# Layer 3's four-bit MLP: two batches rounded together, part of the elementwise work given to GpSimd and ScalarE

## The chip, the cores and the metric

The kernel runs on one core of one Trainium2 chip. The metric is the time of one execution on the device, in microseconds (us), input loads and the store of the output included. Five engines work side by side, each from its own queue in order, and wait for each other by semaphores: TensorE (PE; its weight loads are PEld), VectorE (DVE), ScalarE (ACT), GpSimd (POOL), SyncE (SP, which issues the DMAs). "Idle before" in a row of the profile is time in which the engine stood still.

## What is computed

A decoder of four layers on 8 batches of 112 rows by 256 columns. The change touches only the last stage, the feed-forward part of layer 3, where inputs, hidden values and weights are rounded to four-bit numbers with one scale for each block of 16:

```python
def fake_quant_nvfp4(x, global_scale):
    xb = x.reshape(..., 16)
    amax = max(abs(xb))                      # of each block
    sc8 = round_to_e4m3(clip(amax / 6 * global_scale, 0, 448))
    dq = sc8 / global_scale
    a = clip(abs(xb) / dq, 0, 6)
    return sign(xb) * nearest_fp4(a) * dq

x = x + down(fake_quant(silu(gate(fake_quant(xn))) * up(fake_quant(xn))))   # hidden width 1024
```

## The kernel before

Twelve stages follow each other; `L3Ffn` is the last, and between stages all engines meet (`open_stage`, `close_stage`). Weights are rounded earlier (`FourBitWeights`, in a stage of layer 2, the same helpers at 128 partitions x 2048).

The stage works on ten units of 112 partitions x 1024 floats: `rows` 0 and 1 (the normalized inputs of batches 0 to 3 and of 4 to 7) and `hidden` 0 to 7 (one batch each). `order()` gives the order of steps; each engine's method walks the same list and emits its own part, so a step's place in the list is its place in each engine's queue.

For a unit ("four"), DVE does: the blocks' largest magnitude (L3185, a reduction to 64), nine small operations on 64 numbers a partition that make the scale and its inverse (`four_bit_scales`), and then on 1024 elements: multiply by the inverse scale, clip, take the exponent's bits, make the rounding constant, add it (`four_bit_sums`), and subtract it again (L3373). `Chain` lets each of them wait for the one before (tensor_tensor is L2731, tensor_scalar L2737 or L2735, the reciprocal L2749). POOL multiplies the rounded values by the scale into bf16 (`four_bit_values`, L3176). PE transposes them in 8 blocks (`pe_turn`, L3422), ACT copies them out of PSUM (L3439 for rows, L3444 for hidden), and for a hidden unit PE does the down projection (L259, 8 matmuls of 256 columns), whose result DVE scales and adds to `x` (L3376).

"gate" is, for a batch, eight matmuls of 512 columns on PE (gate into banks 0 and 1, up into banks 2 and 3), ACT's silu of the gate half into `sg` (L3433), and DVE's product with the up half, read from PSUM (L3357). `k.fill` lets PE wait until a bank's reader is done; here banks 0 to 3 are free once DVE's product is.

In the loop over batches DVE's queue is: reduction, small operations, six operations on 1024 elements for batch b, the gate product of batch b + 1, the sum of batch b - 1. `y`, `t`, `hids`, `sc` and `values` are buffers; `t` is a single one.

Of the kernel before, what the change touches and what calls it, by code (L numbers as in the profile page):

```python
# [5 lines left out]
F32 = mybir.dt.float32  # L6
# [41 lines left out]
class Signals:  # L48


    def __init__(self, nc, stack):
# [95 lines left out]
        self.sums_ready = new("sums_ready")  # L147
        self.xl_ready = new("xl_ready")
# [3024 lines left out]
def four_bit_values(k, values, y, sc):  # L3173

    b3 = lambda a: a.rearrange("p (n k) -> p n k", k=16)
    return k.nc.gpsimd.tensor_tensor(b3(values), b3(y),  # L3176
                                     sc[:, 1].unsqueeze(2).broadcast_to([y.shape[0], sc.shape[2], 16]), ALU.mult)


def four_bit_scales(k, src, gs, sc):  # L3180

    c, V, s = Chain(k), k.nc.vector, k.s
    top, s8, c8 = sc[:, 0], sc[:, 1], sc[:, 2]
    V.wait_ge(*s.vstep.now())
    V.tensor_reduce(top, src.rearrange("p (n k) -> p n k", k=16), AX, ALU.max,  # L3185
                    apply_absolute_value=True).then_inc(*s.vstep.up())
# [11 lines left out]
def four_bit_sums(k, src, y, t, sc):  # L3198

    c = Chain(k)  # L3200
    b3 = lambda a: a.rearrange("p (n k) -> p n k", k=16)
    c.tt(b3(y), b3(src), sc[:, 2].unsqueeze(2).broadcast_to([y.shape[0], sc.shape[2], 16]), ALU.mult)
# [3 lines left out]
    c.tt(y, y, t, ALU.add)  # L3206
# [89 lines left out]
class L3Ffn:  # L3296
# [4 lines left out]
    UNITS = (("rows", 0), ("rows", 1)) + tuple(("hidden", b) for b in range(B))  # L3301

    def __init__(self, k):
# [8 lines left out]
        self.values = [take(HID, dt=BF16, parts=S) for _ in range(2)]  # L3312
        self.sg, self.hids = take(HID, parts=S), take(2, HID, parts=S)
        self.hT = take(8, S, dt=BF16)

    def order(self):

        yield "norm", B - 1
        yield "four", 0
        yield "four", 1  # L3320
        yield "turn", 0
        yield "gate", 0
        yield "turn", 1
        for b in range(B):
            yield "four", b + 2
            if b + 1 < B:
# [4 lines left out]
        yield "sum", B - 1  # L3331

    def rows_of(self, n):
        kind, i = self.UNITS[n]
        if kind == "rows":
            half = self.k.row_norms[:, i * HALF:(i + 1) * HALF, :]
            return half.rearrange("p b d -> p (b d)"), self.w["s_in"][0:S, 0:1]
        return self.hids[:, i % 2, :], self.w["s_in"][0:S, 1:2]
# [10 lines left out]
    def dve(self):  # L3349
        k, s, V, st = self.k, self.s, self.nc.vector, self.k.stats  # L3350
        V.tensor_copy(self.ident16, k.ident).then_inc(*s.wq_ready.up())
        for step, i in self.order():
            if step == "norm":
                norm_row_stats(k, i, st, s.stat_ready)
            elif step == "gate":
                V.wait_ge(*s.silu_ready(i + 1))
                V.scalar_tensor_tensor(  # L3357
                    out=self.hids[:, i % 2, :].rearrange("p (h n) -> p h n", h=2), in0=k.banks[0:S, 2:4, :],
                    scalar=self.inv[0:S, 1:2], in1=self.sg.rearrange("p (h n) -> p h n", h=2), op0=ALU.mult,
                    op1=ALU.mult).then_inc(*s.hid_ready.up())  # L3360
            elif step == "four":
                kind, b = self.UNITS[i]
                if kind == "hidden":
                    V.wait_ge(*s.hid_ready(b + 1))
                elif b:
                    V.wait_ge(*s.xn_ready(1))
                if i >= 2:
                    V.wait_ge(*s.quant_ready(i - 1))
                src, gs = self.rows_of(i)
# [313 lines left out]
```

## Time and profile before

| | us |
|---|---|
| median of three runs | 2364.27 (2362.84 to 2365.53) |
| the profiled execution | 2364.53, its span 2363.2 |
| the last stage, in the profile | 2240.9 to 2358.3 |
| DVE busy over the whole span | 1354.9 (57%) |
| PE busy over the whole span | 2043.6 (86%) |

Over the whole span PE is the busiest engine, but the last stage has another balance; the rows below are read from it. The share of each engine in one stage, the queue of its busiest engine and what each of the others waits for tell what a change inside this stage can be worth.

### The profile page before, as it was taken

Reading aid. Unit: us, or ns where it says so; the run is one execution under the profiler, and the core shown is the slowest. Engines: PE = TensorE matmul, PEld = TensorE weight load, DVE = VectorE, ACT = ScalarE, POOL = GpSimd, SP = SyncE. Lnnn points to the kernel's source line nnn. Section 1 sums busy time; section 2 is a strip of 40 time slices with the busy share of each in tenths; the row PEclk is TensorE's granted clock in tenths of the full one; section 3 lists DMA queues with packets and bytes.
Section 4 is the critical chain, followed back from the end, with each engine's and each line's share of the span. In section 5 each row is a group of like instructions: output and inputs, shape, how many; then the busy total and the mean of one; then the engine's idle time right before and its main releaser. Section 6 shows DMA issues by size and latency. Waiting matters only on the chain.

```text
span 2363.2 us, 57229 instructions
## 1 busy us (share of the span) xinstructions
PE 2043.6 (86%) x22720; PEld 1483.5 (63%) x22720; DVE 1354.9 (57%) x3605; ACT 883.8 (37%) x3421; POOL 500.9 (21%) x1131
## 2 busy tenths in 40 slices
PE   7999999998987799897976887999999998789843
PEld 3788888786656566465865654666554544556522
DVE  5666666674335688544644633787263210678797
ACT  2344444443236466211333532666210111246511
POOL 3344444221001100101324511332000000411111
PEclk9655555799989899799997998999999999789966
DMA  3000000104000000300011000000030000000000
GB/s 133 3 5 5 5 4 5 75 2 175 3 1 2 14 12 5 134 1 23 1 48 81 2 1 7 11 8 5 1 148 0 1 0 1 1 14 15 2 0 16
DMA packets 7752, 57.20 MB, mean 24 GB/s; under 512 B 760, under 2 KB 5216, under 8 KB 5728
## 3 DMA queue, kind: packets, MB, share of 16 engines
q1 hardware_dynamic: 7488, 53.54, 5.9%
q8 instruction: 183, 3.00, 0.5%
q14 instruction: 81, 0.66, 0.1%
HBM read 52.62 MB, written 0.92 MB: 23 GB/s over the span
## 4 chain that ended last, share of the span: by engine, by line
PE 66%; DVE 14%; issue 9%; ACT 6%; POOL 4%; DMA 1%; DVEq 0%; POOLq 0%; ACTq 0%; SPq 0%
PE banks L259 42%; PE banks L264 8%; PE banks L1323 6%; PE banks L908 3%; ACT memory L956 2%; DVE memory L1421 2%; PE banks L934 2%; ACT memory L1352 1%; PE banks L1474 1%; ACT memory L1359 1%; DVE memory L1218 1%; DVE memory L795 1%; DVE memory L1427 1%; DVE memory L1430 1%; DVE memory L1439 1%
## 5 line engine op out<-in xcount | busy, mean ns | idle before, releaser
L259 PE MATMUL banks<-memory 128*112 128x256 f32 (+7 forms) x4192 | 1134.2, 427 | 70.7 <-ACT memory L3444 8.0
L259 PEld LDWEIGHTS banks<-memory 128*128 128x128 f32 (+3 forms) x4192 | 708.2, 196 | 401.5 <-issue 258.9
L264 PE MATMUL banks<-memory 112*125 112x112 f32 (+3 forms) x2000 | 305.9, 286 | 123.7 <-DVE memory L795 66.7
L264 PEld LDWEIGHTS banks<-memory 112*125 112x125 f32 (+3 forms) x2000 | 238.6, 172 | 240.3 <-issue 142.9
L1323 PE MATMUL banks<-memory 128*128 128x8 bf16 (+2 forms) x10752 | 325.9, 175 | 25.6 <-DVE memory L1439 5.8
L1323 PEld LDWEIGHTS banks<-memory 128*128 128x128 bf16 x10752 | 304.2, 104 | 48.0 <-DVE memory L1439 45.9
L956 ACT ACTIVATE memory<-banks,memory 112x375 f32<-112x375 f32 x384 | 215.4, 579 | 19.5 <-DVE memory L994 19.1
L994 DVE TENSOR_REDUCE memory<-banks 112x2 f32<-112x750 f32 x192 | 171.0, 933 | 37.0 <-PE banks L908 36.8
L811 POOL TENSOR_TENSOR memory<-memory 112x1 f32<-112x1 f32 x72 | 39.6, 550 | 416.1 <-DVE memory L790 414.6
L1002 DVE COPY memory<-banks 125x448 f32<-125x448 f32 x192 | 116.8, 619 | 11.3 <-PE banks L264 6.9
L1421 DVE TENSOR_REDUCE memory<-banks 128x48 f32<-128x192 f32 x448 | 109.4, 286 | 5.5 <-PE banks L1323 5.5
L908 PE MATMUL banks<-memory 32*112 32x375 f32 x768 | 88.4, 529 | 19.6 <-ACT memory L956 17.4
L1502 ACT ACTIVATE memory<-memory 112x112 f32<-112x112 f32 x192 | 71.7, 374 | 86.1 <-DVE memory L1523 86.1
L1352 ACT ACTIVATE memory<-memory 128x48 f32<-128x48 f32 x224 | 54.4, 243 | 128.1 <-DVE memory L1421 128.1
L978 ACT COPY memory<-banks 125x448 f32<-125x448 f32 x96 | 51.1, 533 | 127.6 <-PE banks L264 127.6
L3142 DVE TENSOR_TENSOR memory<-banks,memory 112x256 f32<-112x256 f32 x8 | 3.4, 424 | 158.4 <-PE banks L259 158.4
L1383 POOL TENSOR_TENSOR memory<-memory 128x16 f32<-128x16 f32 x224 | 48.2, 215 | 206.4 <-DVE memory L1439 206.4
L1201 ACT ACTIVATE memory<-banks,memory 112x112 f32<-112x112 f32 x256 | 86.4, 391 | 9.5 <-DVE memory L1218 8.1
L1366 ACT COPY banks<-memory 128x48 f32<-128x48 f32 x448 | 79.8, 179 | 23.9 <-DVE memory L1400 23.9
L3119 ACT ACTIVATE memory<-banks,memory 128x448 f32<-128x448 f32 x32 | 20.3, 635 | 173.5 <-PE banks L259 173.5
L1439 DVE SCALAR_TENSOR_TENSOR memory<-memory 128x16 f32<-128x16 f32 x224 | 39.2, 175 | 75.7 <-ACT memory L1359 75.7
L956 ACT ACTIVATION_READ_ACCUMULATOR memory<-banks,memory 112x1 f32 x384 | 80.4, 209 | 0.0
(233 smaller groups left out, 2403.8 us busy)
## 6 DMA issues: line engine op xcount, KB each, us to landing
memory<-in_l2x SPq DMA_DIRECT2D x1, 7680.0 KB, 21.5
memory<-in_l2f SPq DMA_DIRECT2D x1, 7168.0 KB, 19.8
memory<-in_l1f SPq DMA_DIRECT2D x1, 4617.0 KB, 14.1
memory<-in_ctxT SPq DMA_DIRECT2D x24, 187.5 KB
memory<-in_l0a SPq DMA_DIRECT2D x1, 4224.0 KB, 16.5
memory<-in_l2f SPq DMA_DIRECT2D x1, 4096.0 KB, 12.8
memory<-in_l3f SPq DMA_DIRECT2D x1, 3073.0 KB, 22.5
memory<-in_l2a SPq DMA_DIRECT2D x1, 3072.0 KB, 18.4
```

The costliest lines, as they stand in the source:

```text
L259: ins = self.nc.tensor.matmul(out, weights[i], acts[i], start=i == 0, stop=i == n - 1)
L264: return self.nc.tensor.transpose(out, in_, self.ident[0:n, 0:n])
L908: ins = PE.matmul(k.bank(bank, S, CK), q, kT, start=True, stop=True)
L956: self.nc.scalar.activation(self.P_both[gi % 2][:, r, :], self.k.bank(r, S, CK), ACT.Exp, bias=u["nmax"][:, 4 * i + r:4 * i + r + 1], scal ...
L994: V.tensor_reduce(u["nmax"][:, 4 * i + 2 * h:4 * i + 2 * h + 2], k.banks[0:S, 2 * h:2 * h + 2, 0:CK], AX, ALU.max, negate=True).then_inc(* ...
L1002: V.tensor_copy(self.PT_both[gi % 2][0:CR, c, :], k.bank(k.at["turn", gi, c], CR, 4 * S)).then_inc(*s.pt_v.up())
L1201: A.activation(self.P_all[:, i, g, :], k.bank(i, S, 4 * S)[:, g * S:(g + 1) * S], ACT.Exp, bias=u["nmax"][:, 4 * i + g:4 * i + g + 1], sca ...
L1323: ins = self.nc.tensor.matmul(own[:, part:3, at:at + B], whh[:, part, l, j, g * P:(g + 1) * P], self.upper[l][:, 0:3 - part, j * B:(j + 1) ...
L1352: A.activation(self.gates[:, l, 1:4, :].rearrange("p g c -> p (g c)"), self.sums[:, l, 0:6 * B], ACT.Tanh).then_inc(*s.act_tanh.up())
L1366: self.nc.scalar.copy(self.slots[l][last][:, 3, :], src).then_inc(*self.s.xw_in.up())
L1421: V.tensor_reduce(self.sums[:, l, first * B:end * B], self.slots[l][last].rearrange("p s c -> p c s"), AX, ALU.add).then_inc(*s.gates_in.up())
L1502: A.activation(weights, weights, ACT.Exp, bias=self.nmax[n % 2][:, at:at + 1], scale=1.0, accum_out=self.total[n % 2][:, at:at + 1]).then_ ...
```

## The change

- `hids`, `y` and `t` become two buffers each of 2048 floats, `sc` two of 3 x 128. Two hidden batches form a pair.
- DVE: the reduction (`four_bit_tops`) stays one for each batch ("hid"); the nine small operations now run once for a pair on 128 numbers ("scale"), as do the multiplication by the inverse scale and the three operations of `four_bit_range` on 2048 elements ("range"). The addition of the rounding constant stays one of 1024 for each batch ("round").
- POOL: the gated product (`up` times `sg`, both in SBUF) in the place of DVE's L3357; the subtraction of the rounding constant for all units but rows 0 and the last; then the values as before, except those of the last unit.
- DVE keeps subtraction and values of the last unit (`last_ready`).
- ACT: after the silu a scaled copy of the up half out of PSUM into `up`; banks 0 to 3 are free once that is done (`up_ready`). `sg` and `up` are single buffers: the next silu waits for POOL's product.
- PE: transposes alternate between banks 4 and 5; `hT` is double. The order of steps is new; POOL's queue is product, product, then for the pair subtraction, values, subtraction, values.

```diff
-        self.y, self.t = [take(HID, parts=S) for _ in range(2)], take(HID, parts=S)
-        self.sc = [take(3, HID // 16, parts=S) for _ in range(2)]
+        two = lambda *dims, dt=F32: [take(*dims, dt=dt, parts=S) for _ in range(2)]
+        self.hids, self.y, self.t = two(2 * HID), two(2 * HID), two(2 * HID)
...
         yield "norm", B - 1
-        yield "four", 0
-        yield "four", 1
+        yield "rows", 0
+        yield "rows", 1
         yield "turn", 0
         yield "gate", 0
-        yield "turn", 1
-        for b in range(B):
-            yield "four", b + 2
-            if b + 1 < B:
-                yield "gate", b + 1
-            if b:
-                yield "sum", b - 1
+        yield "hid", 0
+        yield "gate", 1
+        yield "hid", 1
+        for p in range(HALF):
+            last = p == HALF - 1
+            yield "scale", p
+            if not last:
+                yield "gate", 2 * p + 2
+                yield "hid", 2 * p + 2
+            if p:
+                yield "turn", 2 * p
+            if not last:
+                yield "gate", 2 * p + 3
+            yield "turn", 2 * p + 1
+            yield "range", p
+            if not last:
+                yield "hid", 2 * p + 3
+            yield "round", p
+            if p:
+                yield "sum", 2 * p - 2
+                yield "sum", 2 * p - 1
+        for b in (B - 2, B - 1):
...
         for step, i in self.order():
             if step == "norm":
                 norm_row_stats(k, i, st, s.stat_ready)
...
-            elif step == "gate":
-                V.wait_ge(*s.silu_ready(i + 1))
-                V.scalar_tensor_tensor(
-                    out=self.hids[:, i % 2, :].rearrange("p (h n) -> p h n", h=2), in0=k.banks[0:S, 2:4, :],
-                    scalar=self.inv[0:S, 1:2], in1=self.sg.rearrange("p (h n) -> p h n", h=2), op0=ALU.mult,
-                    op1=ALU.mult).then_inc(*s.hid_ready.up())
-            elif step == "four":
...
+            elif step == "rows":
+                if i:
                     V.wait_ge(*s.xn_ready(1))
...
+                src = k.row_norms[:, i * HALF:(i + 1) * HALF, :].rearrange("p b d -> p (b d)")
+                y, t = self.half(self.y, i), self.half(self.t, i)
+                four_bit_scales(k, src, w["s_in"][0:S, 0:1], self.scales(i))
+                four_bit_scaled(k, src, y, self.scales(i))
+                four_bit_range(k, y, t)
+                self.dve_round(i, i == 0)
+            elif step == "hid":
+                self.dve_hidden(i)
+            elif step == "scale":
+                sc = self.sc[i % 2]
+                if i:
+                    V.wait_ge(*s.quant_ready(2 * i))
+                four_bit_steps(k, w["s_in"][0:S, 1:2], sc)
+                four_bit_scaled(k, self.hids[i % 2], self.y[i % 2], sc)
+            elif step == "range":
+                four_bit_range(k, self.y[i % 2], self.t[i % 2])
+            elif step == "round":
+                self.dve_round(2 * i + 2, False)
+                self.dve_round(2 * i + 3, 2 * i + 3 == self.LAST)
...
+    def dve_hidden(self, b):
+        k, s, V = self.k, self.s, self.nc.vector
+        hid = self.half(self.hids, b + 2)
+        V.wait_ge(*s.hid_ready(b + 1))
+        four_bit_tops(k, hid, self.scales(b + 2)[:, 0])
+
+    def dve_round(self, n, whole):
+
+        k, s, V = self.k, self.s, self.nc.vector
+        y, t = self.half(self.y, n), self.half(self.t, n)
+        V.wait_ge(*s.vstep.now())
+        if not whole:
+            V.tensor_tensor(y, y, t, ALU.add).then_inc(*s.sums_ready.up())
+            return
+        V.tensor_tensor(y, y, t, ALU.add).then_inc(*s.vstep.up())
+        V.wait_ge(*s.vstep.now())
+        V.tensor_tensor(y, y, t, ALU.subtract).then_inc(*s.sums_ready.up())
+        if n == self.LAST:
+            V.wait_ge(*s.sums_ready(n + 1))
+            V.wait_ge(*s.tp16_full(n - 1))
+            four_bit_values(V, self.values[n % 2], y, self.scales(n)[:, 1]).then_inc(*s.last_ready.up())
...
-            elif step == "four":
-                G.wait_ge(*s.sums_ready(i + 1))
-                if i >= 2:
-                    G.wait_ge(*s.tp16_full(i - 1))
-                four_bit_values(k, self.values[i % 2], self.y[i % 2], self.sc[i % 2]).then_inc(*s.quant_ready.up())
+            elif step == "rows" and i == 0:
+                self.pool_values(0)
+            elif step == "hid":
+                G.wait_ge(*s.up_ready(i + 1))
+                if i >= 4:
+                    G.wait_ge(*s.sums_ready(i - 1))
+                G.tensor_tensor(self.half(self.hids, i + 2), self.up, self.sg, ALU.mult).then_inc(*s.hid_ready.up())
+                if i == 0:
+                    self.pool_values(1)
+            elif step == "round":
+                self.pool_values(2 * i + 2)
+                if 2 * i + 3 < self.LAST:
+                    self.pool_values(2 * i + 3)
+
+    def pool_values(self, n):
+        s, G, y = self.s, self.nc.gpsimd, self.half(self.y, n)
+        G.wait_ge(*s.sums_ready(n + 1))
+        if n:
+            G.tensor_tensor(y, y, self.half(self.t, n), ALU.subtract).then_inc(*s.gstep.up())
+            G.wait_ge(*s.gstep.now())
+        if n >= 2:
+            G.wait_ge(*s.tp16_full(n - 1))
+        four_bit_values(G, self.values[n % 2], y, self.scales(n)[:, 1]).then_inc(*s.quant_ready.up())
...
-                        k.fill(o + h, s.hid_ready(i + 1))
+                        k.fill(o + h, s.up_ready(i + 1))
...
-        PE.wait_ge(*s.quant_ready(n + 1))
-        k.fill(bank, read)
+        PE.wait_ge(*(s.last_ready(1) if n == self.LAST else s.quant_ready(n + 1)))
...
                 A.activation(self.sg.rearrange("p (h n) -> p h n", h=2), k.banks[0:S, 0:2, :], ACT.Silu,
-                             scale=self.inv[0:S, 0:1]).then_inc(*s.silu_ready.up())
+                             scale=self.inv[0:S, 0:1])
+                A.activation(self.up.rearrange("p (h n) -> p h n", h=2), k.banks[0:S, 2:4, :], ACT.Copy,
+                             scale=self.inv[0:S, 1:2]).then_inc(*s.up_ready.up())
```

## Rows read from the trace of the kernel before

**Rows 1.** The stage: window, length; busy us of PE, PEld, DVE, ACT, POOL; granted clock.
```profile
2240.90:2358.30 117.40, 49.24 (x208) 31.82 (x208) 106.45 (x181) 19.26 (x19) 21.09 (x12) 0.60 0.00 0
```

**Rows 2.** Groups of the stage by shape: busy us, mean ns, idle before, releaser.
```profile
L2731 DVE TENSOR_TENSOR memory<-memory 112x1024 f32<-112x1024 f32 x20 | 24.5, 1225 | 0.7
L3176 POOL TENSOR_TENSOR memory<-memory 112x1024 bf16<-112x1024 f32 x10 | 19.3, 1930 | 90.6 <-DVE memory L3373 90.6
L2737 DVE TENSOR_SCALAR memory<-memory 112x1024 f32<-112x1024 f32 x20 | 13.9, 694 | 0.7
...
L3185 DVE TENSOR_REDUCE memory<-memory 112x64 f32<-112x1024 f32 x10 | 12.1, 1210 | 0.1
L3357 DVE SCALAR_TENSOR_TENSOR memory<-banks,memory 112x1024 f32<-112x1024 f32 x8 | 10.2, 1277 | 0.0
...
L3433 ACT ACTIVATE memory<-banks,memory 112x1024 f32<-112x1024 f32 x8 | 8.9, 1115 | 34.5 <-PE banks L259 34.5
```

**Rows 3.** Groups by shape, whole span: the same operations at doubled width, in `FourBitWeights`.
```profile
L2731 DVE TENSOR_TENSOR memory<-memory 128x2048 f32<-128x2048 f32 x9 | 20.6, 2292 | 0.3
...
L2737 DVE TENSOR_SCALAR memory<-memory 128x2048 f32<-128x2048 f32 x6 | 7.4, 1227 | 0.2
...
L2749 DVE RECIPROCAL memory<-memory 128x128 f32<-128x128 f32 x3 | 2.9, 954 | 0.1
...
L2737 DVE TENSOR_SCALAR memory<-memory 128x128 f32<-128x128 f32 x9 | 2.4, 268 | 0.3
...
L2731 DVE TENSOR_TENSOR memory<-memory 128x128 f32<-128x128 f32 x6 | 1.8, 293 | 0.2
```

**Rows 4.** Groups by shape of POOL, whole span: f32 tensor_tensor of two plain inputs.
```profile
L2894 POOL TENSOR_TENSOR memory<-memory 128x448 f32<-128x448 f32 x8 | 9.0, 1134 | 27.0 <-ACT memory L2885 27.0
...
L2030 POOL TENSOR_TENSOR memory<-memory 128x224 f32<-128x224 f32 x8 | 5.2, 655 | 22.0 <-DVE memory L1236 22.0
```

**Rows 5.** Timeline, four places where POOL and DVE overlap: start us, duration us, engine.
```profile
986.07 2.23 POOL L2894 TENSOR_TENSOR memory<-memory 128x448 f32<-128x448 f32 x2 [4.20 <-ACT memory L2885]
...
986.64 1.67 DVE L2731 TENSOR_TENSOR memory<-memory 112x32 f32<-112x32 f32 x2
...
2021.88 0.62 DVE L2573 TENSOR_TENSOR memory<-memory 112x448 f32<-112x448 f32 x1 [1.81 <-ACT memory L2536]
...
2021.92 1.57 POOL L2573 TENSOR_TENSOR memory<-memory 112x448 f32<-112x448 f32 x1 [1.23 <-ACT memory L2536]
...
2242.71 1.22 POOL L3170 TENSOR_SCALAR memory<-memory 112x256 f32<-112x256 f32 x1
2243.05 0.26 DVE L2737 TENSOR_SCALAR memory<-memory 112x64 f32<-112x64 f32 x1
...
2251.88 1.93 POOL L3176 TENSOR_TENSOR memory<-memory 112x1024 bf16<-112x1024 f32 x1 [7.94 <-DVE memory L3373]
2252.96 0.90 DVE L2737 TENSOR_SCALAR memory<-memory 112x64 f32<-112x64 f32 x1
```

**Rows 6.** Timeline: the first gate, and the subtraction of the second hidden batch.
```profile
2256.01 3.66 PE L259 MATMUL banks<-memory 128*112 128x512 bf16 x8 [1.05 <-ACT memory L3439]
...
2282.93 1.22 DVE L3373 TENSOR_TENSOR memory<-memory 112x1024 f32<-112x1024 f32 x1
```

**Rows 7.** Timeline of the end, from the last subtraction to the last sum.
```profile
2350.58 1.22 DVE L3373 TENSOR_TENSOR memory<-memory 112x1024 f32<-112x1024 f32 x1
...
2351.89 1.93 POOL L3176 TENSOR_TENSOR memory<-memory 112x1024 bf16<-112x1024 f32 x1 [9.34 <-DVE memory L3373]
...
2353.87 0.93 PE L3422 MATMUL banks<-memory 112*128 112x112 bf16 x8 [7.40 <-POOL memory L3176]
2354.84 0.91 ACT L3444 COPY memory<-banks 128x896 bf16<-128x896 bf16 x1 [10.37 <-PE banks L3422]
...
2355.80 1.95 PE L259 MATMUL banks<-memory 128*112 128x256 bf16 x8 [0.99 <-ACT memory L3444]
2357.79 0.48 DVE L3376 SCALAR_TENSOR_TENSOR memory<-banks,memory 112x256 f32<-112x256 f32 x1 [5.58 <-PE banks L259]
```

More of the change, by code:

```diff
@@ L147, in __init__ @@
         self.sums_ready = new("sums_ready")
+        self.last_ready = new("last_ready")
+        self.up_ready = new("up_ready")
         self.xl_ready = new("xl_ready")
@@ L3170, in norm_row, with four_bit_values, four_bit_tops @@
     return G.tensor_scalar(k.row_norms[:, b, :], k.x[:, b, :], st[:, 6:7], st[:, 9:10], ALU.subtract, ALU.mult)
-def four_bit_values(k, values, y, sc):
+def four_bit_values(engine, values, y, s8):
     b3 = lambda a: a.rearrange("p (n k) -> p n k", k=16)
[L3176 to L3183, printed above, removed]
+    return engine.tensor_tensor(b3(values), b3(y), s8.unsqueeze(2).broadcast_to([y.shape[0], s8.shape[1], 16]), ALU.mult)
+def four_bit_tops(k, src, top):
+    V, s = k.nc.vector, k.s
     V.wait_ge(*s.vstep.now())
@@ L3186, in four_bit_scales, with four_bit_steps @@
                     apply_absolute_value=True).then_inc(*s.vstep.up())
+def four_bit_scales(k, src, gs, sc):
+    four_bit_tops(k, src, sc[:, 0])
+    four_bit_steps(k, gs, sc)
+def four_bit_steps(k, gs, sc):
+    c = Chain(k)
+    top, s8, c8 = sc[:, 0], sc[:, 1], sc[:, 2]
     c.ts(top, top, 1.0 / 6.0, gs, ALU.mult, ALU.mult)
@@ L3198, in four_bit_sums, with four_bit_scaled, four_bit_range @@
 def four_bit_sums(k, src, y, t, sc):
+    four_bit_scaled(k, src, y, sc)
+    four_bit_range(k, y, t)
+    Chain(k).tt(y, y, t, ALU.add)
+def four_bit_scaled(k, src, y, sc):
+    b3 = lambda a: a.rearrange("p (n k) -> p n k", k=16)
+    Chain(k).tt(b3(y), b3(src), sc[:, 2].unsqueeze(2).broadcast_to([y.shape[0], sc.shape[2], 16]), ALU.mult)
+def four_bit_range(k, y, t):
     c = Chain(k)
-    b3 = lambda a: a.rearrange("p (n k) -> p n k", k=16)
-    c.tt(b3(y), b3(src), sc[:, 2].unsqueeze(2).broadcast_to([y.shape[0], sc.shape[2], 16]), ALU.mult)
     c.ts(y, y, 6.0, -6.0, ALU.min, ALU.max)
@@ L3308, in __init__ @@
         self.ident16 = take(P, dt=BF16)
-        self.y, self.t = [take(HID, parts=S) for _ in range(2)], take(HID, parts=S)
-        self.sc = [take(3, HID // 16, parts=S) for _ in range(2)]
+        two = lambda *dims, dt=F32: [take(*dims, dt=dt, parts=S) for _ in range(2)]
+        self.hids, self.y, self.t = two(2 * HID), two(2 * HID), two(2 * HID)
+        self.sc = two(3, 2 * HID // 16)
         self.xT = four_bit_rows(k)
-        self.values = [take(HID, dt=BF16, parts=S) for _ in range(2)]
@@ L3313, in __init__ @@
-        self.sg, self.hids = take(HID, parts=S), take(2, HID, parts=S)
-        self.hT = take(8, S, dt=BF16)
+        self.values = two(HID, dt=BF16)
+        self.sg, self.up = take(HID, parts=S), take(HID, parts=S)
+        self.hT = [take(8, S, dt=BF16) for _ in range(2)]
     def order(self):
         yield "norm", B - 1
-        yield "four", 0
-        yield "four", 1
+        yield "rows", 0
+        yield "rows", 1
         yield "turn", 0
         yield "gate", 0
-        yield "turn", 1
@@ L3340, in run, with half, scales @@
+        for b in (B - 2, B - 1):
+            yield "turn", b + 2
+        for b in (B - 2, B - 1):
+            yield "sum", b
+    def half(self, a, n):
+        pair = a[(n // 2 + 1) % 2]
+        return pair[:, n % 2 * self.HID:(n % 2 + 1) * self.HID]
+    def scales(self, n):
+        return self.sc[(n // 2 + 1) % 2][:, :, n % 2 * self.HID // 16:(n % 2 + 1) * self.HID // 16]
     def run(self):
@@ L3439, in act @@
                     A.copy(self.xT[:, b].rearrange("p k (b s) -> p b k s", b=HALF),
[L3440 removed]
+                           self.turned(4 + i % 2).rearrange("p (b k) s -> p b k s", b=HALF)).then_inc(*s.xT_ready.up())
                 else:
[L3442 to L3444 removed]
+                    if b >= 2:
+                        A.wait_ge(*s.down_full(b - 1))
+                    A.copy(self.hT[b % 2], self.turned(4 + i % 2)).then_inc(*s.h_kept.up())
 def fetch_l0_l1(k):
```

38 lines of the change are left out of this document (9 added, 29 removed).

## Prediction, made before the changed kernel was seen

> **What bounds the kernel now.** Only the last stage changes, so its own rows decide. The busy times of the stage come first: of 117.4 us DVE is busy 106.5, PE 49.2, POOL 21.1, ACT 19.3 [rows 1]. The groups by shape say what DVE does and that it hardly waits (0.7 us before twenty operations), while POOL stood 90.6 us idle for DVE's last operation on a unit [rows 2]. From the subtraction that starts at 2282.93 (second hidden batch) to the one at 2350.58 (the eighth) 67.65 us pass [rows 6, 7]: six batches, 22.55 us a pair, on one full queue. At the end come 6.5 us from the end of the last subtraction (2351.80) to the end of the last sum (2358.27) [rows 7].
>
> **What DVE gives away.** For a pair it loses two gated products of 1.28 and two subtractions of 1.22, 5.0 us. Doubling the width saves little more: one multiplication is 2.29 for twice 1.225, one clip 1.23 for twice 0.69 [rows 2, 3]. What is left for a pair: two reductions 2.42; small operations of 128 numbers, six tensor_scalars (0.23 to 0.27, together 1.45), two tensor_tensors 0.59, one reciprocal 0.95, so 3.0; multiplication 2.29; range 3 x 1.23 = 3.68; two additions 2.45; two sums 0.95 [rows 2, 3, 7]; some 0.3 of gaps and overlaps are over. That is 15.1 instead of 22.55.
>
> **What POOL takes.** Values cost 1.93 [rows 2]. Product and subtraction, 1024 f32 from two plain inputs, are not in the trace. From below: 1.93, the values. From above: 655 ns for 224 and 1134 for 448 are 2.14 ns an element, so 1.134 + 576 x 2.14 ns = 2.37 [rows 4]. I take 2.3, near the plain rows. The Trainium skill (GPSIMD Engine Reference, 3.1 Elementwise) measures 4497 ns for 2048; half of it, 2.25, is an estimate and would shorten the sum by about 0.7 us; no run here shows it. POOL then has per pair 4 x 2.3 + 2 x 1.93 = 13.1 us. Beside DVE's 15.1 that would fit, if the two ran side by side.
>
> **They do not.** Where POOL's values op runs from 2251.88 to 2253.81, DVE's tensor_scalar on 64 numbers, issued at 2252.96, takes 0.90 us instead of 0.26 and ends 0.05 after POOL. Two tiny tensor_tensors beside two POOL operations take 1.67 us, where even 128-wide ones take 0.29 each: one gets through after each POOL operation. The other way round, POOL's 448 elements behind a DVE tensor_tensor take 1.57 instead of 1.13 [rows 3, 4, 5]. So a DVE operation with two inputs in SBUF, or a tensor_scalar, and a POOL operation exclude each other, in order of arrival; only start-up is shared (about 0.15 to 0.2 of a blocked DVE operation, 0.13 of a blocked POOL one). DVE's reductions (memory to memory, one input) and its products out of PSUM keep means of 1.21 and 1.28 though the values op lies beside them in every batch [rows 2]. This is what the change gives up: POOL works now just where it disturbs nobody; afterwards it disturbs clips, additions and small operations. The Trainium skill (SBUF, Who interferes with whom) says that the one that comes second waits out the whole instruction; the rows give back the start-up. By the rule alone, some 20 hand-overs would cost 3 us more, 2379.
>
> **A pair, placed.** Zero is the end of the pair's second addition. POOL: first subtraction to 2.2 (its start-up was over while it waited), beside it the two sums (free). Then values 4.2, second subtraction 6.5, values 8.4, next product 10.7; in each gap one small DVE operation gets through, so five of nine are done at 10.9, the rest, free, at 12.7. Multiplication to 15.0; the other product (its gate: PE until 12.0 behind the transposes and projection that the first values release, ACT until 14.2) waits for it, 17.2; the reduction lies beside it; the first range operation waits until 17.2 and ends at 18.2, the others at 20.75; reduction 21.9, additions 23.1 and 24.3. So 24.3 instead of 22.55: ten of POOL's 13.1 us come on top of DVE's 15.1, and of the rest start-up is most. The last interval has no products and no reductions: about 19.2. Together 24.3 + 24.3 + 19.2 = 67.8 against 67.65: **plus 0.2**.
>
> **The head.** Rows 0 and the first gate stay (PE until 2259.67, silu 1.11 [rows 2, 6]). ACT's copy of up is not in the trace; silu on the same shape is 1.11, and it is hidden wherever POOL is behind; here it is on the path. Then POOL: product 0 from 2262.0 to 2264.3, subtraction and values of rows 1 to 2268.6, product 1 to 2270.9: DVE, done with rows 1 at 2260.9, waits 8 us in all for the two products and reduces batch 1 until 2272.2. Small operations 3.3 and, since product 2 falls into them (second gate done 2265.6, ACT 2267.9; third gate 2271.5, ACT 2273.8), 2.2 more, to 2277.6; multiplication 2279.9; reduction 2281.1; product 3 until 2282.1 delays the range, 2285.9; reduction and two additions 2289.2. Before, the same point was 2284.15: **plus 5.0**.
>
> **The tail.** From the last addition: subtraction of batch 6 on POOL 2.2, values, behind DVE's subtraction of batch 7, to 5.1; DVE's own values of batch 7 are done at 6.2, hidden. But PE takes the two batches in turn: transposes 0.93, copy 0.91, projection 1.95 and their gaps, 3.9, then the same 3.9 for batch 7, and a sum 0.48: 5.1 + 3.9 + 3.9 + 0.5 = 13.4 against 6.5 [rows 7]: **plus 6.9**. Before, the other batch of this pair had gone out 11 us earlier.
>
> Edits with one answer: banks 4 and 5 in turn, the double `hT`, the split of the scales' helper: nothing, PE is busy 49 of 117 us [rows 1]. Banks 0 to 3 are free after ACT's copy rather than after DVE's product; PE waits for DVE anyway. The added waits: behind POOL's wait for `up_ready` stand the values of rows 1 (counted in the head) and later the pair's subtractions, which are due after it anyway; behind DVE's for `hid_ready` stands its whole queue, which the head and the pair count; its wait for `quant_ready` asks for values of two pairs ago.
>
> **The sum.** 5.0 + 0.2 + 6.9 = 12.1. The profiled execution took 2364.53, 0.3 above the median 2364.27; so **2376.4**. With product and subtraction at 1.93, each pair is 1.3 to 1.5 shorter, head and tail 1.5 together: about 5 less, 2371.6.
>
> **The rivals.**
> (a) Exclusion, forecast: slower, 2371 to 2380. For it stand rows of both orders and both kinds of DVE operation [rows 5].
> (b) Faster. DVE and POOL run side by side at this size: Then not DVE's 15.1 but the other product sets the pair. From the end of the first addition: subtraction 2.3, values 4.4, transposes, copy and projection 8.3, gate 11.9, ACT 14.2, product 16.5, reduction 17.7, addition 19.0. So 19.0, 19.0 and 12.6 for the last, 17.0 less than 67.65; in the head product 2 and 3 delay nothing and additions end at 2285.5, plus 1.3; in the tail 1.9 less waiting, plus 5.0: minus 10.7, **2353.8**. It decides if less than about half of POOL's time shuts DVE out. Against it stands the 0.90 for 0.26 [rows 5].
> (c) Between. POOL holds DVE off only in part of an operation: a DVE tensor_scalar issued 0.34 us into POOL's L3170 (1.22) ran in its free 0.26 [rows 5]. That one is a POOL tensor_scalar, with one input. If half of POOL's time is open for DVE, half of the way between (a) and (b): 2365, **no change**.
> (d) The copy on ACT makes table loads (one only for the stage now, copies and silu mixed) or is far longer than 1.11: ACT has 98 us to spare [rows 1], so only the head would feel it; under 2 us, inside (a).
>
> **How the numbers follow.** Chances: (a) 0.76, (b) 0.12, (c) 0.12. A time within 0.2% (4.7 us) can't be told from no change. (a) leaves slower 0.75 and 0.01 for same; so faster 0.12, same 0.13, slower 0.75. The range takes in (a) with its low price of 1.93, a gentler order of arrival at the port (3 us less), and the rule's 2379 with PE's gates and copies a little later (4 more), and reaches down to (c)'s middle: 2364 to 2383.
>
> **What the profile after would show.** Small tensor_scalars of 128 numbers with a mean near 1 us instead of 0.25; POOL's product and subtraction at 2.3 free and about 3 where they wait for an addition; DVE busy more, not less, than 106.5 us; additions of neighbouring pairs 24.3 us apart; 13.4 us from the last plain addition to the last sum. If the small operations show 0.2 to 0.3 and pairs are 19 apart, (b) is true and the argument of the port is wrong; if product and subtraction take 1.9, only a size is off.

## The result and the profile after

The changed kernel takes 2376.47 us (median of five, 2373.76 to 2384.67) against 2365.53 us for the kernel before on the same chip (five, 2362.84 to 2367.57). The ratio is 1.0053, with a 95% interval of 1.0032 to 1.0073: slower, by 10.9 us between the medians. 2376.4 was predicted. Ratios, here and below, are worked out from all runs of both kernels and so are not exactly the quotient of two medians. One later execution of the kernel before took 4326.7 us, in a slow state of the chip, and is left out of every comparison.

The profiled execution is the longest of the five, 2384.67 us, so first one has to see where its time lies. Its span is 2383.3 us, 20.1 longer than the 2363.2 of before. The stage begins with the cast of the identity on DVE, at 2240.92 before and at 2247.95 now: 7.0 us of the 20.1 are there before the first changed instruction. One place at which they arise is a view of five us early in the program, in the same unchanged code (columns as in rows 1: window, length, busy us of PE, PEld, DVE, ACT, POOL, granted clock). Before:

```profile
455.00:460.00 5.00, 5.00 (x47) 4.17 (x48) 3.99 (x10) 3.41 (x17) 1.47 (x2) 1.00 0.01 2
```

After:

```profile
455.00:460.00 5.00, 5.00 (x20) 3.88 (x19) 1.87 (x4) 3.29 (x17) 0.00 (x0) 0.50 0.00 2
```

PE is busy all five us in both, but the granted clock was 0.50 instead of 1.00, the lower instead of the higher of its two levels, and it got through 20 instead of 47 matmuls (the two stretches don't hold quite the same ones). One reciprocal of DVE starts at 451.76 before and at 451.94 after, and the one two rounds of this code later at 464.74 and 468.56. So 3.6 of the 7.0 us arise here, the rest further on in code that is unchanged too. A second profile of the changed kernel (below) has the low clock at this place too (2.2 us lost), but its stage begins 1.0 us earlier than that of before. So such losses come and go with the execution.

What belongs to the change is the stage itself, from that cast to the end of the last sum: 117.35 us before (2240.92 to 2358.27), 130.46 after (2247.95 to 2378.41). Windows of after: the whole stage, and the stage cut at the end of the first pair's additions and at the end of the last plain addition:

```profile
2247.95:2378.41 130.46, 46.82 (x208) 30.17 (x208) 112.74 (x114) 26.95 (x27) 65.39 (x27) 0.57 0.00 0
...
2247.95:2296.45 48.50, 18.92 (x56) 9.00 (x56) 37.92 (x56) 13.57 (x13) 18.99 (x10) 0.54 0.00 0
2296.45:2365.20 68.75, 22.32 (x120) 16.55 (x120) 66.99 (x53) 11.57 (x12) 41.41 (x17) 0.60 0.00 0
2365.20:2378.41 13.21, 5.58 (x32) 4.63 (x32) 7.83 (x6) 1.81 (x2) 4.98 (x2) 0.50 0.00 0
```

Before, the same three parts were 43.23 (2240.92 to the subtraction's end at 2284.15), 67.65 and 6.47 [rows 6, 7]. So the stage grew by 5.3 + 1.1 + 6.7 = 13.1 us. DVE executes 114 instructions in it instead of 181 and is busy for 112.7 us instead of 106.5 [rows 1]: fewer and wider operations, more time (the time for which a started operation is held up counts as busy). The groups of after by shape say which (busy us, mean ns, idle before, releaser):

```profile
L2739 DVE TENSOR_SCALAR memory<-memory 112x128 f32<-112x128 f32 x12 | 13.1, 1092 | 0.3
...
L2733 DVE TENSOR_TENSOR memory<-memory 112x128 f32<-112x128 f32 x8 | 8.5, 1064 | 0.3
...
L2737 DVE TENSOR_SCALAR memory<-memory 112x128 int32<-112x128 int32 x4 | 7.0, 1758 | 0.1
```

The operations on 128 numbers take 1.1 to 1.8 us on average instead of the 0.27 and 0.29 of [rows 3]. The two kinds of POOL work and the copy that moved to ACT, from the same view:

```profile
L3456 POOL TENSOR_TENSOR memory<-memory 112x1024 f32<-112x1024 f32 x8 | 23.3, 2909 | 18.6 <-ACT memory L3519 18.6
L3468 POOL TENSOR_TENSOR memory<-memory 112x1024 f32<-112x1024 f32 x8 | 22.4, 2799 | 28.6 <-DVE memory L3435 28.6
...
L3519 ACT ACTIVATE memory<-banks,memory 112x1024 f32<-112x1024 f32 x8 | 8.9, 1107 | 0.0
```

How a pair runs is read from DVE's and POOL's timeline after the first pair's additions (start, duration):

```profile
2295.39 3.25 POOL L3468 TENSOR_TENSOR memory<-memory 112x1024 f32<-112x1024 f32 x1 [6.27 <-DVE memory L3435]
2296.36 2.36 DVE L2739 TENSOR_SCALAR memory<-memory 112x128 f32<-112x128 f32 x1
2298.72 1.93 POOL L3178 TENSOR_TENSOR memory<-memory 112x1024 bf16<-112x1024 f32 x1
2298.76 4.27 DVE L2737 TENSOR_SCALAR memory<-memory 112x128 f32<-112x128 f32 x2
2300.61 2.34 POOL L3468 TENSOR_TENSOR memory<-memory 112x1024 f32<-112x1024 f32 x1
...
2303.03 1.93 POOL L3178 TENSOR_TENSOR memory<-memory 112x1024 bf16<-112x1024 f32 x1
2303.07 1.97 DVE L2739 TENSOR_SCALAR memory<-memory 112x128 f32<-112x128 f32 x1
2304.91 2.35 POOL L3456 TENSOR_TENSOR memory<-memory 112x1024 f32<-112x1024 f32 x1
2305.07 2.66 DVE L2733 TENSOR_TENSOR memory<-memory 112x128 f32<-112x128 f32 x2
...
2309.55 4.29 POOL L3456 TENSOR_TENSOR memory<-memory 112x1024 f32<-112x1024 f32 x1 [2.29 <-ACT memory L3519]
```

Read the two engines together: from 2295.4 to 2307.3 POOL works through five operations with gaps under 0.1, and one small DVE operation ends just after each of them (a row marked x2 holds two). The last row is the reverse: a product whose free time is 2.34 takes 4.29, since DVE's multiplication of 2048 (2309.34 to 2311.63) came first.

### The profile page after: what moved, and what is told of

The parts are those of the page before. It is cut to its first block, busy times and chain, and to the rows that moved or that the text cites. A ratio compares the mean times of both kernels' runs of the same rounds, so it can differ in the third digit from the quotient of the medians.

```text
span 2383.3 us, 57191 instructions
## 1 busy us (share of the span) xinstructions
PE 2046.1 (86%) x22720; PEld 1483.3 (62%) x22720; DVE 1361.9 (57%) x3538; ACT 890.5 (37%) x3429; POOL 544.6 (23%) x1146
## 4 chain that ended last, share of the span: by engine, by line
PE 66%; DVE 14%; issue 7%; ACT 7%; POOL 5%; DMA 1%; DVEq 0%; POOLq 0%; ACTq 0%; SPq 0%
PE banks L261 42%; PE banks L266 7%; PE banks L1325 6%; PE banks L910 3%; ACT memory L958 2%; DVE memory L1423 2%; PE banks L936 2%; ACT memory L1354 1%; ACT memory L1361 1%; PE banks L1476 1%; DVE memory L1220 1%; DVE memory L797 1%; DVE memory L1429 1%; DVE memory L1432 1%; POOL memory L3468 1%
## 5 line engine op out<-in xcount | busy, mean ns | idle before, releaser
L261 PE MATMUL banks<-memory 128*112 128x256 f32 (+8 forms) x4192 | 1139.4, 428 | 83.7 <-ACT memory L3530 11.9
L958 ACT ACTIVATE memory<-banks,memory 112x375 f32<-112x375 f32 x384 | 215.1, 577 | 20.2 <-DVE memory L996 20.1
L1368 ACT COPY banks<-memory 128x48 f32<-128x48 f32 x448 | 79.9, 179 | 24.3 <-DVE memory L1402 24.3
## 6 DMA issues: line engine op xcount, KB each, us to landing
memory<-in_l2f SPq DMA_DIRECT2D x1, 4096.0 KB, 12.7
```

The lines of the kernel that those rows point to most:

```text
L261: ins = self.nc.tensor.matmul(out, weights[i], acts[i], start=i == 0, stop=i == n - 1)
L958: self.nc.scalar.activation(self.P_both[gi % 2][:, r, :], self.k.bank(r, S, CK), ACT.Exp, bias=u["nmax"][:, 4 * i + r:4 * i + r + 1], scal ...
L1368: self.nc.scalar.copy(self.slots[l][last][:, 3, :], src).then_inc(*self.s.xw_in.up())
```

## The experiments

The theory is the prediction's: two-input DVE operations and tensor_scalars exclude POOL's, in order of arrival, and only the start-up of the one that waits is shared. Its rivals were that the wider operations or the new order cost the time without any such exclusion (the added waits, ACT's copy, the late gates), or that they run side by side. For every run the stage is given (cast of the identity to last sum), since the time ahead of it varies by more than most of what is looked for.

**The two halves of the change apart.** `e1_pairs_only` keeps the wide operations and the new order, and puts product and subtraction back on DVE:

```diff
-        G.tensor_tensor(self.half(self.hids, i + 2), self.up, self.sg, ALU.mult)     # POOL
+        V.scalar_tensor_tensor(out=hid, in0=k.banks[0:S, 2:4, :], scalar=..., in1=self.sg, ...)  # DVE, in dve_hidden
-        G.tensor_tensor(y, y, self.half(self.t, n), ALU.subtract)                    # POOL, in pool_values
+        V.tensor_tensor(y, y, t, ALU.subtract)                                       # DVE, in dve_round
```

> The changed kernel with gated product and subtraction back on VectorE; only the rounding by pairs, the order and the tail are kept. The stage took 117.4 us before and 130.5 after. Theory A (GpSimd and VectorE exclude each other at the memory port, so each moved operation costs VectorE more than it gave back): stage 121 to 122, about 4 us over before, since values of two batches now run one behind the other beside small operations. Rival B (the loss is the pair's latency at head and tail, whoever multiplies): stage 129 to 131, like the changed kernel. Rival C (no exclusion at all): about 110.

`e2_product_pool` puts back the subtraction alone, `e3_subtract_pool` the product alone (with ACT's copy).

> Pairs, product by GpSimd and copy by ScalarE as in the changed kernel, subtraction back on VectorE. A: stage about 123.5 (the subtraction on GpSimd cost some 6 us of the 13). B: 129 to 131. C: about 106.

> Pairs, subtraction by GpSimd as in the changed kernel, product back on VectorE out of PSUM. A: stage about 126.5 (the product on GpSimd cost some 4 of the 13). B: 129 to 131. C: about 103.

Measured, with ratios to the kernel before (2363.26 us beside them): e1 2371.25 us, 1.0041 [1.0026, 1.0056]; e2 2370.90 us, 1.0037 [1.0021, 1.0052]; e3 2377.38 us, 1.0065 [1.0050, 1.0080]. Their stages, in windows of their own traces, first e1:

```profile
2248.35:2369.86 121.51, 49.09 (x208) 31.01 (x208) 109.34 (x130) 18.91 (x19) 22.82 (x11) 0.56 0.00 0
```

e2:

```profile
2241.37:2364.65 123.28, 49.27 (x208) 31.35 (x208) 107.62 (x122) 26.95 (x27) 43.02 (x19) 0.56 0.00 0
```

e3:

```profile
2244.93:2371.04 126.11, 51.15 (x208) 32.14 (x208) 114.23 (x122) 18.91 (x19) 42.30 (x19) 0.55 0.00 0
```

So from 117.35: pairs alone +4.2, the product on POOL 1.8 more (e2 against e1), the subtraction on POOL 4.6 more (e3 against e1), both 9.0 more (after against e1). Each of the three parts costs time; none pays for another, and the two moves together cost 2.6 more than one by one. The subtraction is the dearer of the two. These steps are read from one trace each; the whole times show that each of these kernels is slower than before, but not their order, since the intervals overlap. In e3's timeline the two subtractions and the two values of a pair follow each other on POOL behind the pair's additions, and all of DVE's next small operations meet them; in e2 the first product lies there, but the second lies half beside a reduction.

That pairs alone are slower is worth a look, for they remove thirteen DVE operations for each pair. Timeline of e1, a wait at its head and then one pair:

```profile
2275.73 1.28 DVE L3427 SCALAR_TENSOR_TENSOR memory<-banks,memory 112x1024 f32<-112x1024 f32 x1 [3.71 <-ACT memory L3511]
...
2292.66 1.22 DVE L3438 TENSOR_TENSOR memory<-memory 112x1024 f32<-112x1024 f32 x1
...
2295.22 2.85 POOL L3178 TENSOR_TENSOR memory<-memory 112x1024 bf16<-112x1024 f32 x1 [23.64 <-DVE memory L3440]
2296.31 2.83 DVE L3440 TENSOR_TENSOR memory<-memory 112x1024 f32<-112x1024 f32 x1
...
2299.22 1.93 POOL L3178 TENSOR_TENSOR memory<-memory 112x1024 bf16<-112x1024 f32 x1 [1.16 <-DVE memory L3440]
2299.38 2.12 DVE L2737 TENSOR_SCALAR memory<-memory 112x128 f32<-112x128 f32 x2
...
2315.04 1.23 DVE L3438 TENSOR_TENSOR memory<-memory 112x1024 f32<-112x1024 f32 x1
```

The pair takes 22.38 us (2292.66 to 2315.04) where two single batches took 22.55: 0.2 gained. In the order of before, each values op lay beside a product out of PSUM and a reduction, which it doesn't hold up [rows 2]. In e1 the first lies beside the second batch's subtraction (2.83 instead of 1.22) and the second beside small operations (2.12 instead of 0.49): 3.2 us a pair given back.

That makes a pair as dear as before, not dearer, so the 4.2 us lie at the ends. Cut at the ends of subtractions, as before, e1's stage is 50.79 (head, to 2299.14) + 62.77 + 7.94 (tail, from 2361.91), against 43.23 + 67.65 + 6.47. Two products and reductions, 5.0 us, are done in e1's head instead of behind it. With these counted where they were, the head is 2.6 longer, the six batches 0.1 and the tail 1.5. The head has a wait of 3.71 us that before has not: the pair's small operations need both first products, and the second gate is not ready. In the tail the last two batches go out in turn.

**The exclusion by itself.** Here the kernel before is kept whole, and POOL gets one spare product for each of the ten units, of 1024 f32, out of the rows' norms into a buffer that nobody reads. `e4_spare_range` starts it when the multiplication of the unit is done, so beside the range operations; `e5_spare_product` right behind the values.

```diff
             elif step == "four":
+                G.wait_ge(*s.r_ready(i + 1))          # e4: signalled by the unit's multiplication; e5: absent
...
+                G.tensor_tensor(self.spare, rows[:, 0:1024], rows[:, 1024:2048], ALU.mult)   # e5: behind the values
                 G.wait_ge(*s.sums_ready(i + 1))
```

> The kernel before with one spare GpSimd product of 1024 f32 for each of the ten units, which nobody waits for, issued when VectorE begins its clip, exponent and constant operations. GpSimd is idle there. A: each spare costs VectorE its 2.35 us less the shared start-up of about 0.2, ten of them 21 us: stage 138 to 139, and a tensor_scalar of 1024 behind each spare takes about 2.8 instead of 0.69. C (side by side): 117.4. Half open port: about 128.

> The kernel before with the same ten spare GpSimd products, but each issued right behind the values, so that it starts beside VectorE's product out of PSUM, sum and reduction, which do not use the shared port. A: values 1.93 and spare 2.35 end about 1.35 us after VectorE's port-free work; so about 1.4 a unit for eight units, 2 for the first, nothing for the last: stage 130 to 132, clearly less than the 137.6 measured with the same spares beside the range. If GpSimd's work cost VectorE the same wherever it lies: 137 to 138. Side by side: 117.4.

e4 took 2386.76 us, 1.0102 [1.0075, 1.0130] (two runs; before 2363.26); e5 2376.24 us, 1.0047 [1.0029, 1.0066] (three runs; before 2364.23). Stage and one unit of e4:

```profile
2238.04:2375.63 137.59, 48.27 (x208) 31.75 (x208) 126.69 (x181) 19.24 (x19) 49.56 (x22) 0.60 0.00 0
...
2282.71 2.85 POOL L3393 TENSOR_TENSOR memory<-memory 112x1024 f32<-112x1024 f32 x1 [4.38 <-DVE memory L2731]
2283.39 2.71 DVE L2735 TENSOR_SCALAR memory<-memory 112x1024 int32<-112x1024 int32 x1
```

and of e5:

```profile
2239.15:2369.98 130.83, 49.21 (x208) 31.83 (x208) 119.94 (x181) 19.26 (x19) 44.14 (x22) 0.58 0.00 0
...
2276.30 1.22 DVE L3185 TENSOR_REDUCE memory<-memory 112x64 f32<-112x1024 f32 x1
2277.04 2.35 POOL L3396 TENSOR_TENSOR memory<-memory 112x1024 f32<-112x1024 f32 x1
2277.56 1.88 DVE L2737 TENSOR_SCALAR memory<-memory 112x64 f32<-112x64 f32 x1
```

DVE has the same 181 instructions as before in both, and nobody waits for the spare's result. Ten spares of 2.35 us lengthen the stage by 20.2 us in e4, 2.0 each (the stage is 137.6, where 138 to 139 was expected), and by 13.5 in e5, 1.35 each on average. The difference is the piece that lies beside the reduction, and the tenth spare, behind which DVE has only the last sum. In e5's rows the product starts 0.48 before the reduction's end, and what is left of it is charged to the next tensor_scalar (1.88 instead of 0.25). This is exclusion without any change of order, wait or width, and the rival "side by side", which expects nothing here, is out. So is a port that is open for half of POOL's time: it would have given about 128 for e4.

**POOL's time taken out of the change.** `e7_short_pool` is the changed kernel with product and subtraction on POOL cut to 16 of 1024 columns; it leaves the rest of both out, so its time is that of all waits, orders and widths of the change without POOL's long operations.

```diff
-                G.tensor_tensor(self.half(self.hids, i + 2), self.up, self.sg, ALU.mult)
+                G.tensor_tensor(self.half(self.hids, i + 2)[:, 0:16], self.up[:, 0:16], self.sg[:, 0:16], ALU.mult)
-            G.tensor_tensor(y, y, self.half(self.t, n), ALU.subtract)
+            G.tensor_tensor(y[:, 0:16], y[:, 0:16], self.half(self.t, n)[:, 0:16], ALU.subtract)
```

> The changed kernel with GpSimd's products and subtractions cut to 16 of 1024 columns: every wait, the order and ScalarE's copy stay, only the time at the port goes. It leaves out most of both operations. A: stage 104 to 105, 26 us less than 130.5, and small operations of the pair at their free 0.23 to 0.29 except where values lie beside them. Rival B (latency and the added waits are what costs): 127 to 131.

One run, 2350.65 us; its stage:

```profile
2239.24:2344.39 105.15, 45.13 (x208) 29.79 (x208) 90.22 (x114) 26.97 (x27) 29.84 (x27) 0.61 0.00 0
```

The same instructions (114, 27 and 27 on DVE, ACT and POOL, as after) take 25.3 us less than after's 130.46. So the order, the copy on ACT, the table load and the added waits are not what makes the change slow; without POOL's length it would be 12.2 us faster than before. POOL's busy time falls by 35.5 us (65.39 of after to 29.84), and 25.3 of them were on the path: 71%. This takes away two things at once, the exclusion and DVE's waits for POOL's results; what exclusion costs by itself is shown by e4 and e5.

**A pairing that keeps the cover.** If what e1's pairs give back is the place of the values, a pair whose values stay beside reductions, products and sums should be faster than before. `e6_pairs_amid` has product and subtraction on DVE, pairs the batches 1 and 2, 3 and 4, 5 and 6, leaves 0 and 7 single (so that head and tail stay as before), and issues the rounding of the two halves apart:

```diff
+    GROUPS = ((0,), (1, 2), (3, 4), (5, 6), (7,))
...
...
+            yield "range", g
+            yield "round", here[0]
...
+            yield "tops", coming[0]      # the reduction, and a sum: beside the first values
+            yield "sum", next(sums)
...
+            yield "round", here[1]
...
+            yield "product", coming[1]   # and the next reduction: beside the second values
+            yield "tops", coming[1]
```

> A new order from theory A. Product (out of PSUM) and subtraction stay on VectorE; hidden batches 1+2, 3+4, 5+6 are rounded as pairs, 0 and 7 alone, so head and tail are those of the kernel before; the reductions, products and sums are placed right behind each batch's subtraction, so that GpSimd's values lie beside them. A: a pair takes VectorE about 19.8 instead of 22.55, three of them 8 us, a little lost where values meet a small operation: stage 109 to 111, ratio to before 0.997. Rival B (pairs lose by their latency wherever they lie): stage 117 or more.

2360.56 us (twelve runs) against 2364.23 (eighteen), ratio 0.9980 [0.9969, 0.9991]: faster than the kernel before, if by little, and so than the changed one (1.0053). Stage and one pair:

```profile
2245.34:2358.43 113.09, 45.90 (x208) 28.72 (x208) 102.07 (x142) 19.04 (x19) 21.10 (x12) 0.62 0.00 0
...
2273.81 1.28 DVE L3427 SCALAR_TENSOR_TENSOR memory<-banks,memory 112x1024 f32<-112x1024 f32 x1 [0.96 <-ACT memory L3525]
...
2296.08 1.23 DVE L3463 TENSOR_TENSOR memory<-memory 112x1024 f32<-112x1024 f32 x1
...
2297.39 1.93 POOL L3178 TENSOR_TENSOR memory<-memory 112x1024 bf16<-112x1024 f32 x1 [15.71 <-DVE memory L3463]
...
2298.75 1.65 DVE L3461 TENSOR_TENSOR memory<-memory 112x1024 f32<-112x1024 f32 x1
...
2315.98 1.22 DVE L3463 TENSOR_TENSOR memory<-memory 112x1024 f32<-112x1024 f32 x1
...
2337.99 2.39 DVE L3461 TENSOR_TENSOR memory<-memory 112x1024 f32<-112x1024 f32 x1
```

A pair takes 19.90 us (2296.08 to 2315.98) instead of 22.55; the next one, which has two sums in it like a pair of before, takes 20.08. The tail is as before, since the last batch is single. But the stage missed its 109 to 111: it is 113.1. The rows show the leaks: DVE waits 0.96 and, at the next group, 0.88 us for the gate; an addition behind the sum still takes 1.65 instead of 1.23, twice (2298.75 and 2318.64); and the largest, an addition of the last pair, which has two sums but no reduction ahead of it, takes 2.39. Together these are 3.8 us, and without them the stage would be 109.3. `e8_pairs_amid_later` goes at the two waits and one of the additions of 1.65:

```diff
+            yield "range", g
             if coming:
                 yield "product", coming[0]
-            yield "range", g
...
                 yield "sum", next(sums)
+                if g == 2:
+                    yield "sum", next(sums)
...
-                if g == 2:
-                    yield "sum", next(sums)
```

> Order of e6_pairs_amid with two edits: the gated product of the next group's first batch stands behind the three range operations instead of ahead of them, and two sums instead of one lie beside the first values of the third group. The earlier order's stage took 113.1 us where 109 to 111 were expected; its DVE waited 0.96 and 0.88 us for the gate ahead of the first two range stretches, and an addition behind a sum took 1.65 instead of 1.23 beside POOL's values. Theory A (those places are the miss): the two waits go (1.8 us less) and one of the blocked additions is free again (0.4 less); stage 110.6 to 111.4 us, time 0.995 to 0.998 of the kernel before. Theory B (the miss lies elsewhere, and a wait that is removed comes back behind another operation, since the gate's clock is the limit): stage stays at 112.5 to 113.5.

2357.32 us (six runs) against 2364.98 (nine), ratio 0.9963 [0.9944, 0.9981]. Its stage:

```profile
2237.38:2349.84 112.46, 49.32 (x208) 30.34 (x208) 101.73 (x142) 19.02 (x19) 21.09 (x12) 0.56 0.00 0
...
2273.26 1.28 DVE L3427 SCALAR_TENSOR_TENSOR memory<-banks,memory 112x1024 f32<-112x1024 f32 x1 [1.45 <-ACT memory L3525]
...
2310.62 1.26 DVE L3461 TENSOR_TENSOR memory<-memory 112x1024 f32<-112x1024 f32 x1
```

Neither theory came out whole: 112.46 lies at the low edge of B's range. The blocked addition went (1.26), and both of the gate's waits, but a wait came back behind another operation of the first group, as 1.45 us. That gives (0.96 + 0.88 - 1.45) + (1.65 - 1.26) = 0.8, and the stage is 0.6 shorter than e6's. The wait for the gate in the first group looks like a limit of the chain product, gate, silu and not of DVE's order alone; this is argued from one row. The addition of 2.4 us is still there (2329.39), and so is one of 1.65. The ratio of e8 is lower than e6's by more than 0.6 us would give; their intervals overlap, and the runs don't tell them apart.

**The changed kernel once more.** `e9_after_again` is the changed kernel as it is, for a second profile.

> The changed kernel as it is, profiled a second time. Its first profiled execution had a stage of 130.5 us that began 7.0 us later than that of before, in code that the change does not touch. Theory A (the 7 us are of that execution, not of the change): the stage takes 130.2 to 130.7 us again and begins within 3 us of 2241. Theory B (the change moves something ahead of its stage): the stage begins near 2248 again.

```profile
2239.90:2370.30 130.40, 46.93 (x208) 29.75 (x208) 112.69 (x114) 26.95 (x27) 65.09 (x27) 0.57 0.00 0
```

The stage is 130.40 us again and begins at 2239.90; the execution took 2376.55 us, close to the median of the five (2376.47). The 7.0 us ahead of the stage were of the first profiled execution, not of the change.

## Why the prediction came out

**The exclusion** was read rightly, from rows of 64 and 32 numbers beside operations of 1024 and 448 [rows 5], and it holds at the new sizes. e4, e5 and e7 show it; the order of arrival, one small operation for each POOL operation, stands in after's timeline. Rival (b), 2353.8, fell by the same rows. Its working gave a stage 10.7 us shorter than before, and e7 is 12.2 shorter, but that is no test of (b): in e7 POOL is short, in (b) it runs in full. Rival (c) fell: e4 loses 2.0 us of each 2.35, not half. The row that (c) rested on was read only in part. Behind the tensor_scalar that ran in its free 0.26 beside POOL's L3170 [rows 5] one more ran free (0.20), but the third was held up:

```profile
2243.57 0.41 DVE L2735 TENSOR_SCALAR memory<-memory 112x64 int32<-112x64 int32 x1
```

It takes 0.41 instead of 0.22 (the mean of its ten) and ends at 2243.98, 0.05 after POOL; after shows the same at 2250.60. So this POOL operation shuts DVE out in its later part, after 0.83 us; why not earlier was not tried.

**POOL's price.** 2.3 was taken for product and subtraction between 1.93 and 2.37; free they take 2.34 and 2.35, near the 2.37 of the straight line through the 224- and 448-wide rows [rows 4]. The half of the Trainium skill's figure, 2.25 (GPSIMD Engine Reference, 3.1 Elementwise), is an estimate 4% under it.

**The pair.** From the end of the first pair's additions (2296.45) the placement and the trace run together: POOL's five operations end at 10.8 (10.7 predicted), DVE's small ones at 12.9 (12.7), the multiplication at 15.2 (15.0), the product behind it at 17.4 (17.2), the next additions at 24.7 (24.3). The six batches took 24.71 + 24.71 + 19.33 = 68.75 against 24.3 + 24.3 + 19.2 = 67.8: this term, plus 0.2 in the sum, measured plus 1.1, and was the one that was sized worst. What the rows show beside the placement are gaps of 0.03 to 0.1 us at each hand-over and 0.05 on each POOL operation. One sentence of the prediction is off by its own numbers: 24.3 against 15.1 puts 9.2 of POOL's 13.1 us on top, not ten.

**The head** was predicted at plus 5.0 and measured plus 5.3 (48.50 against 43.23). DVE waits for POOL's two first products as foreseen. The prediction says 8 us in all, but its own placement (2260.9, 2264.3, 2270.9 and a reduction of 1.2) makes 3.4 + 5.4; in after's timeline it is 3.41 + 5.40 = 8.8:

```profile
2268.95 2.34 POOL L3456 TENSOR_TENSOR memory<-memory 112x1024 f32<-112x1024 f32 x1 [8.10 <-ACT memory L3519]
...
2271.32 1.22 DVE L3185 TENSOR_REDUCE memory<-memory 112x64 f32<-112x1024 f32 x1 [3.41 <-POOL memory L3456]
...
2277.94 1.22 DVE L3185 TENSOR_REDUCE memory<-memory 112x64 f32<-112x1024 f32 x1 [5.40 <-POOL memory L3456]
```

Between the two products POOL does the subtraction and the values of the rows, which is why the second wait is the longer. The batch-1 reduction ends 31.2 us after the stage's start; 31.3 was predicted (2272.2 on the clock of before).

**The tail** was predicted at 13.4 and took 13.2 (before 6.5). Timeline of after:

```profile
2364.14 3.25 POOL L3468 TENSOR_TENSOR memory<-memory 112x1024 f32<-112x1024 f32 x1 [9.75 <-DVE memory L3435]
...
2367.47 2.79 POOL L3178 TENSOR_TENSOR memory<-memory 112x1024 bf16<-112x1024 f32 x1
2368.51 2.83 DVE L3178 TENSOR_TENSOR memory<-memory 112x1024 bf16<-112x1024 f32 x1
2370.32 0.93 PE L3506 MATMUL banks<-memory 112*128 112x112 bf16 x8 [12.00 <-POOL memory L3178]
...
2373.99 0.95 PE L3506 MATMUL banks<-memory 112*128 112x112 bf16 x8
```

Exclusion appears here too: POOL's values take 2.79 instead of 1.93 behind DVE's subtraction, and DVE's values 2.83 behind those. The two passes of transposes, copy and projection come 3.7 us apart, where 3.9 was taken.

**The sum.** Foreseen 12.1, measured 13.1 in the stage and 10.9 between the medians. So how close 2376.4 stands to 2376.47 is in part luck: the sum was 1.0 short in the stage, it was added to 2364.27 where the kernel before took 2365.53 beside the changed one, and the medians of the kernel before scatter by more than that from one comparison to the next (2363.26 to 2365.53).

**The Trainium skill's rule** (SBUF — State Buffer, Who interferes with whom) has the second of two contending instructions wait out the whole of the first. By this rule alone 2379 was worked out. In e4, e5 and after's timeline the mechanism is as the Trainium skill states it; the size goes by the rows. In e1, POOL's values behind an addition that ends at 2296.28 end at 2298.07, 1.79 us later and not 1.93: 0.14 of start-up is shared. Over the some 20 hand-overs that the prediction counts this is the 3 us between the rule and the sum.

**The copy on ACT**, rival (d), takes 1.107 us where 1.11 was assumed, and ACT loads one table in the stage, as before.

Not settled: how the 9.0 us of both moves divide where they meet (1.8 and 4.6 alone), whether the wait for the gate in e8's first group and the blocked addition of its last pair can be had back, and what makes a DVE operation one that POOL holds up; none was tried further.

## What to carry to other kernels

Before work is moved from a full DVE to an idle POOL, look for rows in which the two overlap, and sort DVE's operations into those that slow down and those that don't: idle time of POOL is only free beside the second kind, here reductions and reads of PSUM. Doubling the width of DVE's operations saves their start-ups and rearranges what lies beside POOL's work; in e1 the lost cover of the values (3.2 us a pair) ate nearly all that the width saved (0.2 + 3.2), and orders that keep most of the cover (e6, e8) kept most of the gain. And look at the two ends when units are paired: the first pair has to wait for two inputs, and the last one's chains to the output run in turn. In e1 that cost 2.6 us at the head and 1.5 at the tail; in the changed kernel, with POOL's subtraction in the chain as well, the tail grew by 6.7. e6 and e8, with a single first and last batch, have the tail of before.

## What the runs showed of the hardware

- A POOL tensor_tensor that arrives behind a DVE operation of 2048 takes 4.29 us instead of 2.34 (after, 2309.55), and a full POOL queue lets one small DVE operation through after each of its own: six operations of 128 numbers, 1.7 us by [rows 3], took 11.4 (2296.36 to 2307.73).
- DVE's reductions keep their 1.22 us beside POOL's new operations too (2271.32 in after, beside a subtraction of 2.35; 2276.30 in e5), while tensor_scalars, with one input as well, don't (1.88 instead of 0.25 in e5, 2.71 instead of 0.69 in e4). The number of inputs alone doesn't decide.
- POOL's tensor_scalar of 256 numbers (1.22 us) let two small DVE tensor_scalars through in their free time in its first 0.83 us and held up the third until 0.05 after its end (before, 2243.05 to 2243.98).
- Of POOL's extra 35.5 us that after has over e7, 25.3 were on the path. In this stage the second engine's work was for the most part added to that of the first.
- Five us with PE fully busy held 47 matmuls at a granted clock of 1.00 (before) and 20 at 0.50 (after), in nearly the same code. In two executions of the changed kernel the stage began at 2247.95 and 2239.90, 8 us apart, which is more than half of what this change costs; the stage itself repeated to 0.06 us.
